# A program of its own for the second iteration of a pipelined decoder layer, with the cross-attention contexts singly between its steps

## The reference

```
x = x + attn(layernorm(x))      # z = softmax over the SEQUENCE of x W_A^T / 4, 16 heads;
                                # out[i] = sum over j<=i of z[i-j] v[j]: a Toeplitz matrix for each head; then W_O, b_O
x = x + xattn(layernorm(x), ctx)# K = ctx WK, V = ctx WV, Q = x WQ, causal softmax(Q K^T / 16) V
x = x + ffn(layernorm(x))       # 2 shared experts of 128, 16 routed experts of 64, top 2, silu(g) * u, down
```

## Time and profile before

| | |
|---|---|
| median of 3 runs | 573.8 us (572.46, 573.8, 576.2) |
| profiled execution | 573.51 us, its span 571.7 us |
| PE busy | 541.9 us (95%) |
| DVE busy | 426.5 us (75%) |
| ACT busy | 255.7 us (45%) |
| POOL busy | 191.8 us (34%) |
| granted TensorE clock | 1.00 of 2.4 GHz in every slice |

### The profile page before, as it was taken

The page is one execution under the profiler, slowest core; times in us unless marked ns, Lnnn a source line. Parts: engine busy times, 40 slices in busy tenths (PEclk is TensorE's granted clock), DMA queues, the critical chain, the costliest instruction groups (busy, mean ns, idle before and its releaser), DMA issues. The chain is left out here.

```text
span 571.7 us, 12923 instructions
## 1 busy us (share of the span) xinstructions
PE 541.9 (95%) x4716; PEld 368.2 (64%) x4716; DVE 426.5 (75%) x1107; ACT 255.7 (45%) x517; POOL 191.8 (34%) x240
## 2 busy tenths in 40 slices
PE   5787889999999999999999999999999998999997
PEld 4565557566685667766786668666866675666455
DVE  5858687868885787868886888778876776677654
ACT  4565546445354254445344445434543334332332
POOL 4215150223542144223522343234421343133123
PEclk9999999999999999999999999999999999999999
DMA  8995595795439903694449743993189125300351
GB/s 256 308 367 194 182 386 180 155 322 183 112 82 251 335 17 101 148 292 151 111 100 249 242 110 77 204 310 98 51 177 325 57 74 126 64 1 1 86 102 37
DMA packets 90734, 94.70 MB, mean 166 GB/s; under 512 B 28224, under 2 KB 76224, under 8 KB 90432
## 3 DMA queue, kind: packets, MB, share of 16 engines
q1 hardware_dynamic: 90688, 94.09, 58.1%
HBM read 75.66 MB, written 12.12 MB: 154 GB/s over the span
## 5 line engine op out<-in xcount | busy, mean ns | idle before, releaser
L694 POOL TENSOR_TENSOR mid<-gated,mid 128x512 f16<-128x512 f32 x72 | 86.6, 1202 | 214.0 <-ACT mid L880 213.9
L880 ACT ACTIVATE mid<-gated 128x512 f16<-128x512 f32 x72 | 44.9, 624 | 83.3 <-DVEq L1225 80.0
L146 PE MATMUL wide<-w_d,mid 128*128 128x256 f16 x288 | 78.5, 273 | 0.0
L148 PE MATMUL wide<-w_d,mid 128*128 128x256 f16 x288 | 78.5, 273 | 0.0
L147 PE MATMUL wide<-w_d,mid 128*128 128x256 f16 x288 | 78.5, 272 | 0.0
L1203 DVE SCALAR_TENSOR_TENSOR gated<-gated,score 128x512 f32<-128x512 f32 x72 | 49.1, 682 | 37.6 <-ACT gated L875 37.5
L146 PE MATMUL rows<-h3T,w_gu 128*128 128x512 f16 x160 | 60.7, 379 | 0.3 <-DVEq L126 0.3
L146 PE MATMUL score<-h3T,w_gu 128*128 128x512 f16 x160 | 60.7, 379 | 0.2
L147 PE MATMUL rows<-h3T,w_gu 128*128 128x512 f16 x160 | 60.6, 379 | 0.0
L148 PE MATMUL rows<-h3T,w_gu 128*128 128x512 f16 x160 | 60.6, 379 | 0.0
L148 PE MATMUL score<-h3T,w_gu 128*128 128x512 f16 x160 | 60.6, 379 | 0.0
(11 more groups left out here) (249 smaller groups left out, 1402.8 us busy)
## 6 DMA issues: line engine op xcount, KB each, us to landing
toep<-z_scratch SPq DMA_DIRECT2D x14, 2048.0 KB, 18.3
stage<-comb_scratch SPq DMA_DIRECT2D x32, 512.0 KB, 8.5
toep<-z_scratch SPq DMA_DIRECT2D x4, 1024.0 KB, 11.2
x_bo<-in_x SPq DMA_DIRECT2D x8, 512.0 KB, 11.8
x_in<-in_xr SPq DMA_DIRECT2D x7, 512.0 KB, 11.1
qT<-q_scratch SPq DMA_DIRECT2D x7, 512.0 KB, 3.9
vx<-v_scratch SPq DMA_DIRECT2D x7, 512.0 KB, 5.2
out<-x_out SPq DMA_DIRECT2D x7, 512.0 KB, 3.0
```

What stands on the lines that cost most here:

```text
L146: pe.matmul(out, stationary[0], moving[0], start=start, stop=False, **kw)
L148: return pe.matmul(out, stationary[1], moving[0], start=False, stop=stop, **kw)
L694: pool.tensor_tensor(mid_slot(j, 1, late), gate_slot(j, late), mid_slot(j, 0, late), ALU.subtract).then_inc(mid_split.sem, 1)
L880: act.activation(mid_slot(j, 0, late), gate_slot(j, late), ACT.Copy).then_inc(mid_hi.sem, 1)
```

## The change

- `second_iteration` on PE, ACT, DVE and POOL replaces what `iteration` did for it = 1. On PE the product for z and both value projections now stand ahead of the Toeplitz products (before: one ahead, two between and behind them). The contexts' units, before partly in groups of two to four, stand mostly singly between the steps.
- The four pieces of gu_r are done later, one at a time: ACT scales the float32 in place, then copies to hi (two instructions, `part_scaled`), and POOL subtracts (before: one on ACT, one on DVE).
- SP issues both halves of gu_r behind the Toeplitz rows of batch 0, after the residual and a context (before: one half ahead of these rows).
- scores(0..3) use s0, s1, g3 and s2, that is both banks in turn.
- Batch 2 gets a pair of its own, in `gated` and `h1p`; batch 3 takes the pair that was batch 2's, batch 5 the old one of batch 3. The wait of batch 5 for the stores of batch 2 falls away; a wait for them comes into iteration 2 on ACT.
- x of batch 2 is normalised by ACT (scale and bias), before by DVE.

The diff, cut to its core:

```diff
-CONTEXT_AT = {5: (4, (0, 1)), 6: (4, (2, 3)), 7: (5, (0, 1)), 8: (5, (2,))}
-CONTEXT_BEFORE = {3: (3, (2,)), 4: (3, (3,))}
-SAME_PAIR = {5: 2, 6: 4, 7: 6}
+SAME_PAIR = {6: 4, 7: 6}
...
+        LATE = len(pieces) - LATE_PIECES
+        GATES_2 = LATE - 4
...
+        def score_use(it, c):
+            return ("s0", "s1", "g3", "s2")[c] if one_group(it) else f"s{c}"
...
 sync:
-                    if not m:
-                        load_gates(0)
...
                     sp.wait_ge(first_toep_loaded, 32)
+                    load_residual(it)
+                    load_context(2)
+                    load_gates(0)
                     load_gates(1)
-                    load_context(2)
...
 gpsimd:
+            def second_iteration(it):
+                add_bias(it - 1)
+                part_context_columns(2)
+                reciprocal_deviation(it - 1, 1)
+                make_shift(it - 1)
+                part_context_columns(3)
+                part_weights(range(GATES_2, LATE))
+                part_context_columns(4)
+                reciprocal_deviation(it + 1, 0)
+                make_shift_x(it + 1)
+                reciprocal_deviation(it - 1, 2)
+                reciprocal_deviation(it - 1, 2, 1)
+                part_context_columns(5)
...
 scalar:
+            def part_scaled(i):
...
+                act.activation(src, src, ACT.Copy, scale=X_W).then_inc(w_scaled, 1)
+                act.wait_ge(w_scaled, i - GATES_2 + 1)
+                act.activation(dst[:, 0, k, at], src, ACT.Copy).then_inc(w_hi, 1)
...
+            def second_iteration(it):
+                part_context(1, (0, 1))
+                part_weights(range(MIDDLE, GATES_2))
+                for g in range(K2):
+                    take_first_mix(g)
+                part_values(it, it, 0)
+                part_values(it, it, 2)
+                part_turned(it, it - 1, mixT, mixT_hi, "mix")
+                part_context_columns(2)
+                part_context(1, (2, 3))
+                z_powers(it)
+                part_scaled(GATES_2)
+                part_context(2, (0,))
+                part_context_columns(3)
+                part_context(2, (1,))
+                normalise_last(it - 1, it)
+                part_context(2, (2,))
+                part_turned(it, it - 1, h2T, h2T_hi, "h2")
+                part_context(2, (3,))
+                part_scaled(GATES_2 + 1)
+                act.wait_ge(w_lo, GATES_2 + 1)
+                part_context(3, (0,))
+                exp_scores(it, it - 1, 0)
+                exp_scores(it, it - 1, 1)
+                part_z(it)
+                part_scaled(GATES_2 + 2)
+                part_context(3, (1,))
+                act.wait_ge(ctx_stored[1], 32)
+                part_prob(it, it - 1, 0)
+                exp_scores(it, it - 1, 2)
+                part_scaled(GATES_2 + 3)
+                part_context(3, (2,))
+                part_prob(it, it - 1, 1)
+                exp_scores(it, it - 1, 3)
+                part_context_columns(4)
+                part_context(3, (3,))
+                part_prob(it, it - 1, 2)
+                part_context(4, (0,))
+                part_prob(it, it - 1, 3)
+                part_context_columns(5)
+                part_context(4, (1,))
+                act.wait_ge(w_lo, LATE)
+                part_context(4, (2, 3))
+                normalise_x(it + 1)
+                part_turned(it, it - 1, h3T, h3T_hi, "h3")
+                part_context(5, (0, 1))
+                part_turned(it, it + 1, h1T, h1T_hi, "h1")
+                part_context(5, (2, 3))
...
 vector:
+            def second_iteration(it):
...
+                part_z(it)
+                part_context(3, (1,))
+                part_prob(it, b, 0)
+                score_max(it, b, 2)
+                x_statistics(it + 1, range(2))
+                score_sum(it, b, 2)
+                part_context(3, (2,))
+                score_max(it, b, 3)
+                part_prob(it, b, 1)
+                attended(it, 0)
...
+                part_context(4, (1,))
+                attended(it, 3)
+                attended_statistics(it, 2)
+                aggregate(b, 2, attended_statistics(it, 3), 1)
+                normalise(b, it, 2, x_res, h3)
+                part_context(4, (2,))
+                normalise(b, it, 2, x_res, h3, 1)
+                part_context(4, (3,))
...
 tensor:
+            def second_iteration(it):
+                z_product(it)
+                project(it, "v0", h1T, w_v)
+                project(it, "v2", h1T, w_v)
...
+                    toeplitz(it, b, g)
+                pe.wait_ge(mix_taken, K2)
+                turn(it, "mix", h2)
+                context(1, (2, 3))
+                project_mix(it)
+                context(2, (0, 1, 2))
+                turn_halves(it, "h2", h2, h_ready[1], b, h2_normed)
+                context(2, (3,))
+                context(3, (0,))
...
+                scores(it, 0)
+                scores(it, 1)
+                context(3, (1,))
+                turn_probs(it, b, 0)
+                scores(it, 2)
+                context(3, (2,))
+                turn_probs(it, b, 1)
+                attend(it, 0)
+                scores(it, 3)
+                context(3, (3,))
+                turn_probs(it, b, 2)
+                attend(it, 1)
+                context(4, (0,))
+                turn_probs(it, b, 3)
+                attend(it, 2)
+                context(4, (1,))
+                attend(it, 3)
+                context(4, (2, 3))
+                turn_halves(it, "h3", h3, h_ready[2], b)
+                context(5, (0, 1))
...
+                turn(it, "h1", x_in)
+                context(5, (2, 3))
```

More of the change, by code:

```diff
@@ L928, in iteration @@
             def iteration(it, f, m, d, n, c=None):
[L929 to L932, removed]
+                if f and m and not d:
+                    second_iteration(it)
+                    return
                 if c == 6:
@@ L1340, in x_statistics, with add_residual @@
                     aggregate(b, 0, last)
-            def iteration(it, f, m, d, n, c=None):
-                first = f and m and not d
-                if first:
-                    part_context(1, (0, 1))
-                    rows.take(dve, it, "v0")
-                    part_weights(range(MIDDLE, len(pieces) - LATE_PIECES - 2))
+            def add_residual(it, k):
+                if not k:
+                    dve.wait_ge(x_biased.sem, x_biased.at(it - 1, 1))
+                    dve.wait_ge(x_kept.sem, x_kept.at(it - 2, 1))
+                rows.take(dve, it, f"o{k}")
+                dve.wait_ge(rows.ready.sem, rows.is_ready(it, f"o{k}"))
+                dve.scalar_tensor_tensor(x_res[:, k:k + 2], rows.bank(f"o{k}")[:].rearrange("p (c e) -> p c e", c=2),
+                                         1 / (X_MIX * X_W), x_bo[:, k:k + 2], ALU.mult,
+                                         ALU.add).then_inc(rows.taken.sem, 1)
+                hold(dve, rows.taken, rows.is_taken(it, f"o{k}"))
+                return statistics(1, x_res, range(k, k + 2))
@@ new lines, in attended_statistics @@
+            def attended_statistics(it, c):
+                hold(dve, turned.taken, turned.is_taken(it, f"p{c}"))
+                return statistics(2, x_res, [c])
+            def second_iteration(it):
+                b = it - 1
+                rows.take(dve, it, "v0")
+                part_context(1, (0, 1))
+                part_weights(range(MIDDLE, GATES_2))
+                z_max(it)
+                part_values(it, it, 0)
+                part_values(it, it, 2)
+                rows.take(dve, it, "o0")
+                part_turned(it, b, mixT, mixT_hi, "mix")
+                turned.take(dve, it, "h2.0")
+                part_context(1, (2, 3))
+                add_residual(it, 0)
+                aggregate(b, 1, add_residual(it, 2))
+                part_context(2, (0,))
+                normalise(b, it, 1, x_res, h2)
+                z_invert(it)
+                score.take(dve, it, "s0")
+                part_context(2, (1, 2))
+                part_turned(it, b, h2T, h2T_hi, "h2")
+                part_context(2, (3,))
+                for c in range(2):
+                    score_max(it, b, c)
+                part_context(3, (0,))
+                for c in range(2):
+                    score_sum(it, b, c)
+                part_z(it)
[8 more added lines that the diff above has]
+                attended(it, 0)
+                score_sum(it, b, 3)
+                attended_statistics(it, 0)
+                part_context(3, (3,))
+                part_prob(it, b, 2)
+                attended(it, 1)
+                x_statistics(it + 1, range(2, C))
+                part_context(4, (0,))
+                part_prob(it, b, 3)
+                aggregate(b, 2, attended_statistics(it, 1))
+                attended(it, 2)
+                part_context(4, (1,))
[6 more added lines that the diff above has]
+                part_context(4, (3,))
```

(15 more changed lines are left out.)

186 lines of the change are left out of this document (56 added, 130 removed).

## The result

The changed kernel took 579.27 us (median of 6 runs, 578.22 to 579.88), the kernel before 573.52 in the same rounds (6 runs, 572.46 to 576.2): ratio 1.0088, 95% interval 1.0067 to 1.0108. It is 0.9% slower, where I had forecast no change to be measured and 573.0, and outside the range of 569.0 to 577.3. The profiled execution took 578.22 us with a span of 576.4, against 573.51 and 571.7.

The account below looks back on a forecast made before the run. Chains between engines, not any engine's work, were taken to bound the second iteration (10.7 us of PE idle). A 4.5 us lead shrinks to 0.7 us overall: 573.5 - 0.7 = 572.8, 573.1 on the median's scale, stated 573.0; range 569.0 to 577.3.

Parts of the forecast that it names:

- the first of the walk: Toeplitz products, second iteration: begin at 33.5 us, end at 39.1, with half of an unexplained 1.0 us issue gap kept.
- the walk: Step-by-step timing of the new order in the second iteration, from Toeplitz products to the next ones; 0.7 us gained in all.
- the wait of 1.18: PE's wait for the second half of the Toeplitz rows, 1.18 us, claimed to go as less data is queued ahead.
- my upper bound: Issue gap inside the Toeplitz products: taken as half of 1.0 us, with bounds 0 and 1.0.
- the 57: Second iteration's attention: first scores expected near 55 us; a start after 57 would show the prediction wrong.
- waits of 1.6, 2.8 and 2.2 us: PE's new waits in the attention: ahead of attend(0), of turning probability 2, and of unit (4,0).
- the rule of the Trainium skill: DVE and POOL contention on four gate pieces: up to 1.1 us of DVE time by the rows, near nothing by the rule.
- 0.9 us from this reciprocal to the second half of h3: End of the second iteration: rstd at 79.7 us, second half of h3 ready at 80.6.
- the lead: PE's gain by the first scores, 4.5 us; 1.5 left at attend(1), nothing left after attend(3).
- The rival in which the lead is kept: Attention: ACT's pieces fall into its waiting time, so the 4.5 us lead comes through, 569.3 us; chance 0.17.
- The slower rival: POOL late with context columns of batches 4 and 5, pieces over 3 us: 3.5 us slower, 577.3; chance 0.14.

Follow-up runs that it names:

- experiments 5 to 7: 5: changed kernel plus 64 short matmuls around the Toeplitz products' lead-up, 573.66 us; 6: kernel before plus the same, 573.72; 7: changed kernel with 3.5 MB of loads later, 575.28.
- The fillers: Changed kernel plus unread matmuls of 128 columns in PE's idle time ahead of attend(0), turning of probability 2 and unit (4,0); 577.51 us, ratio 1.0064.
- experiment 8: Changed kernel plus both the 64 short matmuls ahead of the Toeplitz products and the fillers in the attention's waits; 574.1 us, ratio 1.0005.
- shift: Changed kernel plus 64 short matmuls, results unread, in PE's idle time ahead of the Toeplitz products; 573.66 us, ratio 0.9998.
- experiment 3: Changed kernel with load order and gate pieces as before (ACT copy, DVE subtraction, none in the attention); 575.45 us, ratio 1.0023.
- before_banks: Kernel before with only scores 2 and 3 of the second iteration moved to g3 and s2; 573.41 us, ratio 0.9999.
- before_shift: Kernel before plus the same 64 short matmuls at the same two places as in shift; 573.72 us, ratio 1.0001.
- combined_shift: Changed kernel with gate pieces and load order as before, context columns of batches 4 and 5 split earlier, plus 64 short matmuls; 567.78 us, ratio 0.9888.
- best: Kernel of combined_shift with gate pieces 11 and 12 later on ACT and DVE; 566.26 us, ratio 0.9872.

## Why the prediction was wrong

**The step that failed** is the first of the walk: "Another 1.0 us in them is put down to issue; nothing in the trace explains it, so I take half of it (bounds 0 and 1.0)", together with "so the wait of 1.18 goes". I counted the wait for the rows as won and halved the gap, as if they were apart. But the gap was a wait for instructions, and the wait for the rows had hidden part of it. The wait for the rows went, and the gap grew to 1.96 us, above my upper bound (experiments 5 to 7). In the profile that is 1.5 us over my figure, and the clock, which fell behind it, made turning the mix last 1.76 us instead of 0.9 and the two units 3.2 instead of 2.6: the W_O product began at 46.59, not 43.45. The first scores came at 58.18, past the 57 that the prediction names as a sign of being wrong.

**The clock was missing from the sum.** The profile before had it full everywhere, and I forecast waits of 1.6, 2.8 and 2.2 us within 10 us of one another without asking what they would do to it. From 71.9 to 78.7 us it was at 0.50; (4,0) took 2.54 us instead of 1.31, and PE, 2.8 us behind my walk at that unit's start, was 4.9 behind at the end of attend(3) (81.70 against 76.8). The fillers show that idle time brings it, and experiment 8 the price, 2.3 us in the attention.

**POOL's shared time was argued away.** I weighed the rule of the Trainium skill ("SBUF", "Who interferes with whom") only for the gate pieces, and found their price near nothing. The same section lists tensor_scalar among the VectorE operations that can enter a two-port mode and then exclude GpSimd, and the normalisation of h3, a TENSOR_SCALAR on float32, is what met POOL's columns: both start behind the same reciprocal. The walk gave 0.9 us from this reciprocal to the second half of h3. The two blocks alone took 2.40 us, 1.7 more than without POOL and 0.8 more than in the kernel before. Of this 0.6 came through to PE's (5,0), as that unit waited for the columns anyway; moving them won 1.2 us. By this the trace agrees with the Trainium skill, though no row shows which mode DVE was in, and I had weighed the wrong pair of instructions.

**What held.** With the gap taken away (`shift`), the walk can be laid beside the run: W_O product 43.13 (43.45 forecast), first scores 54.72 (54.85), attend(1) 67.74 (68.5), unit (4,0) 70.69 (71.4). So up to there the lead was won and given back where it was said, by ACT's scaled pieces ahead of unit (3,1) and of (3,2) (experiment 3), and by POOL's columns of batch 4. The rival in which the lead is kept is out. The slower rival named POOL with the columns, by pieces of 3 to 4 us; they took 2.13, so its mechanism wasn't there, and the slower result came from another. The 573.0 is met by `shift` with 573.7, but in part by luck: its iteration 2 begins at 92.04 us, where the walk had 90.45 and the kernel before 91.19, and what follows is 0.65 us shorter than before. The changed kernel does not meet it, as the place of its instructions was no part of my sum.

Of the 5.7 us between the medians, 5.6 go with the shift; the profiled pair shows 3.3 of these in the second iteration (95.36 against 92.04) and 1.2 behind it, 0.7 of that in the wait for the transposed mix of iteration 2 (0.90 against 0.20 us). The rest, 1.1 us, lies between the profiled execution (578.22), the fastest of the changed kernel, and its median. The profiled one had a mean granted clock of 0.991, the other five 0.987 or 0.988, so they were at the lower level for longer. By the profiles of the variants this is most likely the stretch in the first iteration, which costs some 0.5 us there and is absent with the short matmuls. That is an estimate, and what is left I can't place.

## What to carry to other kernels

A wait for data can hide part of a wait for instructions, and taking it away uncovers the other: price each wait by what would be late next, and never halve one that the trace cannot explain. A gap with "issue" behind it is to be laid beside the packets of the instruction queue. Before an order is judged, count the instructions up to a gap that stays in every variant; if the count is the same, move it with a few cheap instructions or thin out the transfers there. And an order that bunches short waits of TensorE is to be charged for its clock as well as for the waits.

## What the runs showed that I had not expected

- PE stood still behind its 342nd matmul in the kernel before (1.0 us), in `before_banks` (0.9) and in the changed one and its five variants without a shift or late loads (1.88 to 2.40 us), and nowhere near it with 64 matmuls more ahead, or with 93 instead of 414 GB/s of DMA traffic. Sixty-four useless matmuls made a kernel 1% faster.
- The granted clock went from 2.4 to 1.2 GHz for 3.4 or 6.8 us in the midst of the kernel: behind the gap of 1.96 us, behind the wait of 2.48 us that 2.10 us follow, and, where these were filled, behind the wait of 2.27 us for h3; in `before_shift` behind the wait of 1.98 us for the rows. It wasn't so each time: in `shift` the same wait for h3, 2.28 us, brought nothing, nor did the wait of 2.29 us in `combined_shift`. In `before_banks`, with no wait of PE over 1.43 us in the second iteration, and in `best` (1.34) it never fell there.
- A profile with the clock full everywhere is one execution. Of the 57 executions of the kernel before in the three groups, 16 had a mean granted clock of 0.999 or 1.0 (median 573.2 us), 32 one of 0.996 or 0.997 (573.7) and nine less (574.6).
- Two TENSOR_SCALAR instructions on float32 took 0.71 us alone, 1.54 to 1.64 beside POOL instructions of 0.72 us and 2.40 beside those of 1.15 us.
